# Removing the filler products of TensorE between the membrane scan and the first attention tiles

## The reference

```python
h = _layernorm(x, axis=-1) * (1 + ca) + sa
# r, ek, v: three projections of h; wkv: two linear scans over the tokens
mem = BETA * mem + inp_t - reset * THRESH      # the membrane scan, nonlinear in mem
spk = spike_fn(mem - THRESH)                   # 1 where the membrane is over the threshold
x = x + ga * spk
h = _layernorm(x, axis=-1) * (1 + cb) + sb
# two blocks: local attention (8 heads of 64, windows of 64), then a gated MLP
x = x + gb * _L0_ffn_ref(h, ...)
```

## Time and profile before

| | |
|---|---|
| median of 3 runs | 572.86 us (572.21 to 574.23) |
| time of the profiled execution | 573.93 us |
| its span, first to last instruction | 572.1 us |
| mean granted TensorE clock over the span | 0.949 of 2.4 GHz |
| busy: TensorE, VectorE, ScalarE, GpSimd | 491.3, 437.4, 347.6, 316.3 us |
| filler products (L1470) | 40 |

### The profile page before, as it was taken

How to read it: one execution, slowest core, us unless ns; L and a number is a source line. 1 busy time by engine, 2 the same in 40 slices (tenths; PEclk the granted TensorE clock), 3 DMA queues, 4 the chain that set the end, 5 groups by cost and what they waited for, 6 DMA issues and landing times. The chain is left out here.

```text
span 572.1 us, 11749 instructions
## 1 busy us (share of the span) xinstructions
PE 491.3 (86%) x4026; PEld 309.5 (54%) x4026; DVE 437.4 (76%) x1179; ACT 347.6 (61%) x1001; POOL 316.3 (55%) x257
## 2 busy tenths in 40 slices
PE   4741037889999999999989999999999998999995
PEld 4311013457777776543457777776544445667774
DVE  6699997879999995546899999995445687457775
ACT  4771002679999997543479999997646525533331
POOL 6551008788888888576888888884010275110000
PEclk9795558989999999999999999999999999999999
DMA  8400002221111112000031111111000000000000
GB/s 290 153 1 1 1 1 75 47 46 40 38 40 39 38 40 69 16 1 1 1 111 41 38 39 34 35 38 38 1 2 0 0 1 1 1 0 19 21 18 19
DMA packets 14832, 19.93 MB, mean 35 GB/s; under 512 B 2314, under 2 KB 8948, under 8 KB 14644
## 3 DMA queue, kind: packets, MB, share of 16 engines
q1 hardware_dynamic: 14484, 19.08, 12.2%
q10 hardware_dynamic: 288, 0.08, 0.1%
HBM read 8.94 MB, written 1.05 MB: 17 GB/s over the span
## 5 line engine op out<-in xcount | busy, mean ns | idle before, releaser
L515 ACT ACTIVATE prob<-psS,nmx 128x128 f32<-128x128 f32 x256 | 89.9, 377 | 19.8 <-DVE nmx L1114 19.8
L809 POOL TENSOR_TENSOR rn<-ssq,half 128x16 f32<-128x16 f32 x32 | 93.2, 2911 | 4.0 <-DVE ssq L1100 1.1
L801 POOL TENSOR_TENSOR ra<-ra,rb 128x512 f32<-128x512 f32 x64 | 80.1, 1273 | 2.7 <-DVE rb L1082 2.7
L652 POOL TENSOR_TENSOR rst<-mv,half 128x4 f32<-128x4 f32 x24 | 25.3, 1053 | 73.9 <-DVE mv L903 62.6
L1459 PE MATMUL psQK<-wqkv,hsA 128*128 128x512 f32 x128 | 62.2, 605 | 1.6 <-DVE hsA L1063 1.2
L515 ACT ACTIVATION_READ_ACCUMULATOR prob<-psS,nmx 128x1 f32 x256 | 55.4, 216 | 0.0
L1079 DVE TENSOR_TENSOR ra<-psQK,rope 128x512 f32<-128x512 f32 x64 | 43.9, 686 | 6.6 <-PE psQK L1459 5.9
L817 POOL TENSOR_TENSOR qkn<-ra,rn 128x512 f32<-128x512 f32 x32 | 33.3, 1042 | 26.4 <-DVE qkn L1108 26.4
L1114 DVE TENSOR_REDUCE nmx<-psS 128x4 f32<-128x512 f32 x64 | 41.1, 683 | 3.5 <-PE psS L1564 3.4
L1082 DVE TENSOR_TENSOR rb<-psQK,rope 128x512 f32<-128x512 f32 x64 | 43.6, 681 | 0.0
L633 ACT ACTIVATE gel<-psQK 128x512 f32<-128x512 f32 x32 | 19.1, 596 | 39.8 <-PE psQK L1772 39.8
(11 more groups left out here) (238 smaller groups left out, 1203.7 us busy)
## 6 DMA issues: line engine op xcount, KB each, us to landing
vAB<-vAB SPq DMA_DIRECT2D x62, 128.0 KB, 2.2
wqkv<-in_wqkv SPq DMA_DIRECT2D x2, 768.0 KB, 8.2
big<-in_x SPq DMA_DIRECT2D x4, 256.0 KB, 4.6
ropeb<-in_rope SPq DMA_DIRECT2D x1, 1024.0 KB, 6.4
big<-in_ew SPq DMA_DIRECT2D x2, 512.0 KB, 4.2
out<-big SPq DMA_DIRECT2D x4, 256.0 KB, 2.3
wmod<-in_wmod SPq DMA_DIRECT2D x2, 384.0 KB, 5.9
w<-in_w SPq DMA_DIRECT2D x2, 341.0 KB
```

The costliest lines, as they stand in the source:

```text
L515: act.activation(prob[:, k, :], psS[:, hb, c * P:(c + 1) * P], ACT.Exp, bias=nmx[:, k:k + 1], accum_out=sums[:, n % 2, k:k + 1]).then_inc( ...
L801: pool.tensor_tensor(o, o, rb[:, r], ALU.add).then_inc(s["sum_" + name], 1)
L809: pool.tensor_tensor(rn[:, :], ssq[:, :], half[:, :], ALU.pow).then_inc(s["rn_ready"], 1)
```

## The change

All six calls of `keep_clock` go. The helper stays and is no longer called. No wait, no real product and no other engine's list is touched; the order of the real work on TensorE stays as it is.

```diff
             pe.wait_ge(s["dve_b"], 1 + 2 * SEQ * (PASSES - 1) + SEQ)
-            keep_clock(12, psO[:, 0, :])
             pe.wait_ge(s["init"], 3)
             pe.wait_ge(s["mod_raw"], 1)
             pe.wait_ge(s["cnt_ready"], 1)
             mm(psT1[0:1, 0:1], cnt[:, 0:1], ones[:, :], start=True, stop=True).then_inc(s["cnt_sum"], 1)
-            keep_clock(10, psO[:, 0, :])
...
             stack_t1(0)
             stack_t1(1)
-            keep_clock(2, psT1[:, :])
             stack_t1(2)
-            keep_clock(8, psT1[:, :])
             stack_t1(3)
             ln_t2(ln_no(1, 0))
-            keep_clock(4, psT1[:, :])
             pe.wait_ge(s["ld_wq"], 16)
             pe.wait_ge(s["edges"], 4)
             proj_part(0, 0, 1)
             ln_t2(ln_no(1, 1))
             proj_part(0, 0, 0)
             ln_t2(ln_no(1, 2))
             proj_qk(0, 1)
-            keep_clock(4, psT1[:, :])
```

## The result

The changed kernel takes 575.09 us (median of 17 runs, 573.70 to 575.97), the kernel before 572.86 us (17 runs beside them, 571.48 to 574.23): ratio 1.0039, 95% interval 1.0030 to 1.0049. It is slower by 2.2 us. The forecast was 574.7 in a range of 572.7 to 576.2.

The account below looks back on a forecast made before the run. VectorE's scan bounds until 85 us, then the groups' chain, then the VectorE-GpSimd loop. A 0.68 head start and low clock at first k and q gave +1.25: 575.2 or 574.1 by base, 574.7 taken, range 572.7 to 576.2.

Parts of the forecast that it names:

- The place and the first half of the sum: Group 3 to first projection: without the 8 products, statistics 0.9 us earlier and the projection at 99.44, a gain of 0.68.
- The covers named for the 12, 10 and 2 products: Groups 0 to 2: GpSimd's spikes and additions until 95.49 hide transposes 0.45 us slower each, so 0 on the path.
- the sign: Clock at 0.50 without a break from 42 us to between 102.6 and 106, named as showing the forecast right.
- The penalty: First k and q products: low clock turns 2.15 us of stream into 4.3; range +0.8 to +1.35, taken +1.3.
- its terms (1.3 and 0): +1.3 for low clock at the first k and q products, 0 for the later low stretch; sum given as +1.25.
- The carry to the end: From GpSimd's first root at 105.55 on, the VectorE-GpSimd loop starts 1.3 later; last instruction about 1.2 later.
- a bound of 0.2: Low stretch at 117.4 to 120.8: costs the loop at most 0.2 us; term 0, bounds -0.2 and +0.1.
- Rival A: TensorE's queue is the bound; without the later fall it regains up to 1.6 us: 573.1 us, chance 0.13.
- Rival B: Group 3's transposes: not slower, the 0.68 gain stays if the clock rises by 100.8: 572.5 us, chance 0.10.
- C: Clock low until the stream is dense at 117.57: +3.7 on top of +1.25, 578.4 us, chance 0.09.
- The two readings of the 1.07 us: Profile's excess over the median: either the profiler's (574.1) or median executions without the clock's fall (575.2); 574.7 taken.
- The rule for throttled time: Penalty is throttled length times share of pulses lost: 13.6 us added low time costs 6.8, to about 580.7.

Follow-up runs that it names:

- after_again: The changed kernel, without any of the six calls, run unchanged once more for a second trace: 574.35 us (1 run).
- scan_only: Only the first two filler calls (12 and 10) stay, the other four of the kernel before left out: 574.94 us, ratio 1.0042 to it.
- hold_again: Second measurement of filler counts 12, 10, 13, 9, 9, 4 in place of the kernel before's 12, 10, 2, 8, 4, 4: 572.39 us, ratio 0.9989.
- hold_pro: Same filler counts as hold_again plus 14 idle products in the prologue, against the kernel before: 572.37 us, ratio 1.0002.
- before_4: The kernel before, unchanged, run for another trace: 571.36 us (1 run).

## Why the prediction was right

**The place and the first half of the sum** held. Group 3's transposes with the data (-1.42), its statistics 0.9 earlier, the first projection 0.68 earlier: measured -0.91 and -0.69. The covers named for the 12, 10 and 2 products held: without them GpSimd adds group 3's spikes 8.24 us behind the mark (92.70), as before (94.23), though the sets of transposes take longer. That the clock would stay low until then held too. The ground for it was weak, as the products of the row that I went by are of another kind, 2 columns wide:

```profile
44.66 2.72 PE L1417 MATMUL psO<-silc,wmod 128*128 128x2 f32 x12 [5.31 <-DVE big L954]
```

The rise came at about 102, which is 103.6 counted from the mark of before, inside the 102.6 to 106 that were named as the sign.

**The penalty** was 2.15 us of stream doubled, less the head start. q's rotation was to be 1.35 later, with 1.3 taken: it is 1.36 in the profiled execution. The sum then has 1.25 where its terms (1.3 and 0) make 1.3; nothing in it accounts for the 0.05. The term is a little too small: with the low level under all of q's product (after_again) the first root is 1.52 later than before's 19.56. I said that after every start in the rows but one the level rose within 3.9 us; in after_again it took 6.

**The carry to the end** held within 0.15: 1.35 at the first root, 1.20 from tile 3 on, 1.23 at the last instruction. The 0.15 is given back between the first root and tile 3, 25.57 us before and 25.42 after, where a bound of 0.2 stood for the fall at 117, which the changed kernel's trace lacks. The other traces fit in the main: 25.42 without that fall (scan_only), 25.53 to 25.68 in ten with it, before's among them. But hold_again and hold_pro have 25.42 with a fall that comes at least 0.5 us sooner behind the first root, so its place seems to count too. after_again has the fall, and there nothing is given back (1.52 at the first root, 1.62 at tile 3).

**Rival A** was put to its own test by that. Its condition came true, the clock didn't fall in the later pause and TensorE had its 1.6 us back (from tile 1's transposes at 117.57 and 117.38 to the first of `prob`, at 121.36 and 119.60), and the lateness stayed 1.20. The VectorE-GpSimd loop is the pace, 29.32 us for four tiles in both. **Rival B** is refuted by the rise at about 102 us, and **C** likewise: dense work from the first projection on raised the clock long before 117, in after_again too (by 104.2).

**The two readings of the 1.07 us** were the uncertain part, and I took the middle, so that the forecast lies 0.4 from the median is partly luck. The runs lie on the side of the second, that executions without the fall pull the median of before down: before_4 is one. But the profiled execution of before was also late in its prologue, by up to 1.4 us against others, which I did not see; part of the 1.07 is probably that.

**The rule for throttled time** (the Trainium skill, "TensorE: Matmul & The Clock Gate", section "Terms") would have made 6.8 us of the 13.6 that I had added. From 40 to 125 us the two traces have a granted clock of 0.70 before and 0.64 after, so some 10 us more at the low level (the fall at 117 is gone), which by the rule is 5. The measured 2.2 doesn't agree with it here: in most of that time TensorE had nothing to do, and low time without work cost nothing. Where work on the path filled the time, it does agree: from the start of k's product to the rise are 4.1 us, which makes 2.1 by the rule, and the lateness grew by 2.05, from -0.69 to +1.36.

## What to carry to other kernels

Filler products earn their time only if the clock is up when the first dense, waited-for products come. What counts is the last pause before them, not the long idle stretch ahead: here 4 small fillers there were worth about 60% of all 40, and 22 beside and behind the scan, alone, nothing. Size a filler for its pause at the low level, in the shortest form that the pause takes in any execution; a filler that outlives its pause is a delay (8 products at the low level, 3.54 us, kept group 3's transposes waiting for 1.4, and the one in the prologue the first product for 1.6).

When two traces are to be compared and the clock wanders, compare from a common mark and not from the start. Take several traces: one in five of the kernel before had another course, with 1.3 us between the two, and by the runs it may be one in two.

## What the runs showed of the hardware

The same pause of 2.53 us, after the same work, was followed by a fall to 1.2 GHz in four executions and by none in a fifth. From the start of dense work, the rise to 2.4 GHz came after 4.1 us in one execution of the changed kernel and after 6 in the other. One and the same program thus differs by 1.3 us between executions in this stretch alone, and the kernel before by another 1.4 in its prologue (spikes' start 84.58 to 85.99; 1.6 over all kernels with this prologue); the runs of before spread over 2.5 to 3.0 us in each session.
